# The first expert layer of a two-layer graph network: two phases with weights in two parts, on one Trainium2 core

## The reference, cut to what matters

```
x = x + _L0_ffn_ref(_layernorm(x), w1, b1, w2, b2, wr, br)
...
logits = xf @ wr + br
topk_vals, topk_idx = jax.lax.top_k(logits, K)             # K = 2 of E = 4
gates = jax.nn.softmax(topk_vals, axis=-1)
h = gelu(einsum('nd,edh->enh', xf, w1) + b1)               # 1024 -> 512
y = einsum('enh,ehd->end', h, w2) + b2                     # 512 -> 1024
c = einsum('eh,ehd->ed', gelu(b1), w2) + b2
out = einsum('nk,nkd->nd', gates, y_sel - c_sel + c.sum(axis=0))
```

## Time and profile before

| what | us |
|---|---|
| median of 3 runs | 2559.07 (2556.42 to 2559.77) |
| the profiled execution's own time | 2577.34 |
| its span, first to last instruction | 2575.3 |
| mean granted TensorE clock (share of full speed) | 0.971 |
| PE / DVE / ACT / POOL busy | 2397.2 / 1564.5 / 920.4 / 887.0 |

### The profile page before, as it was taken

The page is one execution under the profiler, slowest core; times in us unless marked ns, Lnnn a source line. Parts: engine busy times, 40 slices in busy tenths (PEclk is TensorE's granted clock), DMA queues, the critical chain, the costliest instruction groups (busy, mean ns, idle before and its releaser), DMA issues.

```text
span 2575.3 us, 29106 instructions
## 1 busy us (share of the span) xinstructions
PE 2397.2 (93%) x9625; PEld 1694.6 (66%) x9625; DVE 1564.5 (61%) x2417; ACT 920.4 (36%) x1629; POOL 887.0 (34%) x843
## 2 busy tenths in 40 slices
PE   6989998969999979999999999999999898977997
PEld 3543334634444458788888888887778676866785
DVE  8737776421142376645545555558889889766555
ACT  4012223311111233221221221228789896533333
POOL 2757774001111035655600000034346552213443
PEclk9999999979999989999999999999999999988998
DMA  4026676273343275454354354268678794457864
GB/s 155 1 97 205 205 208 172 111 255 100 109 126 98 65 258 192 171 193 143 123 192 144 121 191 151 106 237 258 212 250 295 273 344 161 142 181 285 325 217 169
DMA packets 195723, 466.10 MB, mean 181 GB/s; under 512 B 29352, under 2 KB 30152, under 8 KB 195608
## 3 DMA queue, kind: packets, MB, share of 16 engines
q1 hardware_dynamic: 101192, 219.34, 24.8%
q0 software_dynamic: 64272, 190.20, 23.1%
q10 hardware_dynamic: 30144, 55.12, 5.7%
HBM read 370.23 MB, written 99.96 MB: 183 GB/s over the span
## 4 chain that ended last, share of the span: by engine, by line
PE 76%; DMA 9%; DVE 6%; issue 4%; POOL 2%; ACT 2%; DVEq 0%; SPq 0%; ACTq 0%; POOLq 0%
PE pair L1292 8%; PE pair L1294 8%; PE pair L1293 8%; PE pair L1172 6%; PE pair L1192 6%; PE pair L1079 4%; DMA tok_x<-x_rows,tok_list 3%; PE pair L1310 3%; PE pair L1039 3%; PE pair L1313 3%; PE pair L1058 3%; PE pair L1330 3%; PE pair L1331 2%; PE pair L1332 2%; DMA tok_raw<-in_L_ffn_w 2%
## 5 line engine op out<-in xcount | busy, mean ns | idle before, releaser
L1471 ACT ACTIVATE sq_h<-quad 128x512 fp32r<-128x512 f32 x196 | 123.1, 634 | 453.6 <-PE pair L1294 448.8
L932 POOL DMA_INDIRECT rows_y<-y_rows,l_row x184 | 208.4, 1133 | 209.9 <-PE pair L1313 182.2
L1292 PE MATMUL pair<-sq_h,xh 128*128 128x512 f32 x700 | 273.3, 390 | 2.7 <-DVE sq_l L2294 2.7
L1294 PE MATMUL pair<-sq_l,xh 128*128 128x512 f32 x700 | 273.0, 390 | 0.0
L1293 PE MATMUL pair<-sq_h,xl 128*128 128x512 f32 x700 | 272.9, 390 | 0.0
L2382 DVE SCALAR_TENSOR_TENSOR low_y<-rows_y,l_inv,high_y 128x1024 fp32r<-128x1024 f32 x184 | 234.1, 1284 | 47.1 <-ACT high_y L1471 46.8
L1471 ACT ACTIVATE high_y<-rows_y,l_inv 128x1024 fp32r<-128x1024 f32 x184 | 210.4, 1144 | 40.9 <-PE pair L1313 27.5
L909 POOL DMA_INDIRECT inv_ring<-inv_count,at_ring x184 | 189.9, 1032 | 70.8 <-issue 52.5
L872 POOL DMA_INDIRECT XT<-h_rows,l_src x184 | 178.8, 972 | 70.0 <-issue 37.5
L2294 DVE TENSOR_TENSOR sq_l<-quad,sq_h 128x512 fp32r<-128x512 f32 x196 | 131.6, 696 | 97.8 <-ACT sq_h L1471 97.0
L1079 PE MATMUL pair<-XT,XN 128*128 128x504 f32 x368 | 188.8, 636 | 0.0
(11 more groups left out here) (369 smaller groups left out, 5055.6 us busy)
## 6 DMA issues: line engine op xcount, KB each, us to landing
quad<-in_L_gnn_weight SPq DMA_DIRECT2D x28, 1024.0 KB, 5.6
xh<-sum_parts SPq DMA_DIRECT2D x14, 1280.0 KB, 7.6
xl<-sum_parts SPq DMA_DIRECT2D x14, 1280.0 KB, 11.4
y_rows<-u ACTq DMA_DIRECT2D x70, 256.0 KB, 2.3
tok_raw<-in_L_ffn_w SPq DMA_DIRECT2D x8, 2048.0 KB, 13.5
tok_raw<-in_L_ffn_w SPq DMA_DIRECT2D x16, 1024.0 KB, 14.4
exp_bg<-bias_gelu_rows SPq DMA_DIRECT2D x23, 512.0 KB, 5.0
x_rows<-X SPq DMA_DIRECT2D x20, 512.0 KB, 6.5
```

The source lines that it names most:

```text
L932: pool.indirect_dma_start(rows_y[s % RING1][:], None, y_rows, bass.IndirectOffsetOnAxis(ap=l_row8[:, s:s + 1], axis=0)).then_inc(y_in[s % ...
L1292: mm(o, high[:, k, :], sq_h[:, k, :], start=(k == 0), stop=False)
L1294: last = mm(o, high[:, k, :], sq_l[:, k, :], start=False, stop=(k == KE - 1))
L1471: return nc.scalar.activation(dst, src, func, **kw)
```

## The change

The layer becomes two loops over the 23 slots. In the first PE makes all up products; ACT copies the raw product to `exp_h`, PE transposes it, DVE adds the bias on the transposed row (the bias is now one number per partition and slot, picked from a small table ahead of the loop), ACT takes the gelu and stores the slot's 128x512 hidden tile to `hidden_rows` in memory over its own DMA queue. In the second SP loads each hidden tile back (`load_hidden`), DVE takes gelu(b1) off (`take_bias`), ACT makes its high part (`hidden_parts`), DVE its low part (`hidden_low`), PE makes the down product, ACT copies it out (instead of DVE) into one of two buffers, POOL scatters it. Both products are made of three float32r matmuls. The gathered rows get a high part on ACT (`expert_x`) and a low part on DVE. Weights are split piece by piece (`expert_high` on ACT, `expert_low` on DVE, 64 pieces each, 128x512) into three places: w1 of experts 0, 1, 2 ahead of the loop or at its start, w1 of expert 3 at slot 9 into expert 0's place, w2 of expert 0 at slots 20 and 21, w2 of expert 1 right behind the last up product, w2 of expert 2 at slots 0 and 1 of the second loop, w2 of expert 3 at its slot 9. The constant row is summed in two banks of PSUM, a quarter at a time (first loop, slots 4 to 7 and 13 to 16; second loop, slots 2 and 3, and 4 to 7), copied out by ACT at slot 8 and summed by PE behind slot 9. The bias broadcasts, and the small transpose and store that fed them, go. The split of the first relation weight moves to slots 20 and 21 of the second loop.

```diff
-        exp_w = place("exp_w", "xt", [P, E0, 2, 8, HALF])
+        exp_raw = [place(f"exp_raw{i}", r, [P, 8, HALF], skip=8 * HALF) for i, r in enumerate(("xt", "u"))]
+        exp_tail = [place(f"exp_tail{h}", r, [P, KH, HALF], skip=16 * HALF) for h, r in enumerate(("xt", "u"))]
+        exp_w = place("exp_w", "xt", [P, 3, 20, HALF], F32R)
+        exp_x = place("exp_x", "os", [P, 3, 2, KH, P], F32R)
...
+        exp_hr = [place(f"exp_hr{b}", "xn", [P, KH, P], skip=D + b * HID) for b in range(2)]
+        exp_hp = [place(f"exp_hp{b}", r, [P, 2, KH, P], F32R, skip=n) for b, (r, n) in enumerate((("xn", 0), ("os", D)))]
+        exp_out = [place(f"exp_out{b}", r, [P, D]) for b, r in enumerate(("b2", "os"))]
+        c_kept = place("c_kept", "xt", [P, D], skip=16 * HALF)
...
+            def load_hidden(s):
+                sp.wait_ge(*hid_stored(s))
+                if s < 2:
+                    sp.wait_ge(exp_x_full, 2 * NT + 2 * (ESLOTS - 2) + 2)
...
+                    sp.wait_ge(exp_hl_ready, 1 + s - 1)
+                sp.dma_start(exp_hr[s % 2][:].rearrange("p c n -> p (c n)"), hid_dram[s]).then_inc(hid_in[s % 2][0], 16)
...
             sp.wait_ge(slot_summed, RING0 + SLOTS)
-            expert_half(0, 1)
+            first_weights(0, raw[:])
...
+            first_weights(1, exp_raw[1][:])
+            sp.wait_ge(a_full, A_ROUTE + len(TOKG))
+            first_weights(2, exp_raw[0][:])
+            sp.wait_ge(*exp_rows_here(0))
+            sp.wait_ge(*exp_rows_here(1))
+            sp.wait_ge(exp_wl_ready, 8)
+            first_weights(3, raw[:])
+            second_weights(0, tails)
+            sp.wait_ge(exp_wl_ready, 32)
+            second_weights(1, raw_halves)
+            load_hidden(0)
+            load_hidden(1)
+            sp.wait_ge(c_part_ready, 1)
+            sp.wait_ge(exp_wl_ready, 40)
+            second_weights(2, tails)
+            for s in range(2, ESLOTS):
+                load_hidden(s)
...
+            for s in range(2, ESLOTS):
+                pool.wait_ge(exp_x_full, 2 * NT + 2 * s - 2)
+                gather_expert(s)
...
+            def expert_up(s, j, at):
+                if j == 0:
+                    if s < 3:
+                        pe.wait_ge(exp_wl_ready, 8 * (s + 1))
+                    if s >= 2:
+                        pe.wait_ge(exp_h_ready, s - 1)
+                pe.wait_ge(exp_xl_ready, 2 * s + j + 1)
+                o = up_bank[s % 2]
+                high, low = exp_x[:, (2 * s + j) % 3, 0, :, :], exp_x[:, (2 * s + j) % 3, 1, :, :]
+                for c in range(KH):
+                    k = 4 * j + c
+                    if s == ONE_EXPERT:
+                        pe.wait_ge(exp_wl_ready, 24 + k + 1)
+                    w_high, w_low = (exp_w[:, bass.ds(at, 1), n, :].rearrange("p o n -> p (o n)") for n in (k, 8 + k))
+                    mm(o, high[:, c, :], w_high, start=(k == 0), stop=False)
+                    mm(o, low[:, c, :], w_high, start=False, stop=False)
+                    last = mm(o, high[:, c, :], w_low, start=False, stop=(k == KD - 1))
+                    if k == KD - 1:
+                        last.then_inc(exp_up_full, 1)
+                    elif s in (ONE_EXPERT - 1, ESLOTS - 1):
+                        last.then_inc(exp_piece_free, 1)
...
+            def expert_down(s, h, at):
+                if h == 0:
+                    if s == 0:
+                        pe.wait_ge(exp_wl_ready, 40)
+                    pe.wait_ge(exp_hl_ready, 1 + s + 1)
+                if s >= 2:
+                    pe.wait_ge(exp_out_ready, 2 * (s - 2) + h + 1)
+                elif s == 1:
+                    pe.wait_ge(exp_h_ready, ESLOTS - 1)
+                o = exp_down[s % 2][h]
+                high, low = exp_hp[s % 2][:, 0, :, :], exp_hp[s % 2][:, 1, :, :]
+                for k in range(KH):
+                    piece = h * KH + k
+                    if s in (1, 2, ONE_EXPERT):
+                        pe.wait_ge(exp_wl_ready, {1: 40, 2: 48, ONE_EXPERT: 56}[s] + piece + 1)
+                    w_high, w_low = (exp_w[:, bass.ds(at, 1), n, :].rearrange("p o n -> p (o n)") for n in (piece, 8 + piece))
+                    mm(o, high[:, k, :], w_high, start=(k == 0), stop=False)
+                    mm(o, low[:, k, :], w_high, start=False, stop=False)
+                    last = mm(o, high[:, k, :], w_low, start=False, stop=(k == KH - 1))
...
+            pe.wait_ge(exp_at_ready, 1)
+            expert_rows(0)
+            expert_rows(1)
+            for s in range(ESLOTS):
+                at = place_of(exp_up_at, s)
+                for j in range(2):
+                    if s + 1 < ESLOTS:
+                        expert_rows(2 * s + 2 + j)
+                    expert_up(s, j, at)
+                    if j == 0 and s >= 1:
+                        expert_hidden(s - 1)
+            for s in range(ESLOTS):
+                at = place_of(exp_down_at, s)
                 for h in range(2):
-                    if s >= 1:
-                        pe.wait_ge(exp_out_ready, 2 * s + h - 1)
-                    for k in range(KH):
-                        last = mm(down_bank[h][:], exp_hT[:, k, :], exp_w[:, bass.ds(exp_index[s % 2], 1), 1, h * KH + k, :].rearrange("p o n -> p (o n)"),
-                                  start=(k == 0), stop=(k == KH - 1))
-                    last.then_inc(exp_down_full, 1)
-
-            pe.wait_ge(exp_of_ready, 1)
-            expert_rows(0)
-            for s in range(ESLOTS):
-                expert_up(s)
-                if s + 1 < ESLOTS:
-                    expert_rows(s + 1)
-                if s >= 1:
-                    expert_down(s - 1)
-                expert_hidden(s)
+                    expert_down(s, h, at)
+                    if s == 0 and h == 0:
+                        expert_hidden(ESLOTS - 1)
...
+            def expert_high(src, at, pieces):
+                for k in pieces:
+                    copy(exp_w[:, at, k, :], src[k]).then_inc(exp_wh_ready, 1)
...
+            for e, at in ((1, 1), (2, 0)):
+                act.wait_ge(exp_w_in[e], 16)
+                expert_high([exp_raw[at][:, k, :] for k in range(KD)], at, range(KD))
+
+            def expert_x(n):
+                act.wait_ge(exp_x_full, 2 * NT + n + 1)
+                copy(exp_x[:, n % 3, 0, :, :], tx_bank[n % 2][:].rearrange("p (q n) -> p q n", q=4)).then_inc(exp_xT_ready, 1)
+
+            def keep_h(s):
+                act.wait_ge(exp_up_full, s + 1)
+                if s >= 1:
+                    act.wait_ge(exp_h_full, s)
+                copy(exp_h[:], up_bank[s % 2][:]).then_inc(exp_h_ready, 1)
+
+            def store_h(s):
+                act.wait_ge(exp_hm_ready, s + 1)
+                nc.scalar.activation(exp_hT[s % 2][:], exp_hT[s % 2][:], ACT.Gelu).then_inc(exp_gelu_ready, 1)
+                act.wait_ge(exp_gelu_ready, s + 1)
+                act.dma_start(hid_dram[s], exp_hT[s % 2][:].rearrange("p c n -> p (c n)")).then_inc(hid_out[s % 2][0], 16)
+
+            def hidden_parts(s):
+                act.wait_ge(exp_hb_ready, 1 + s + 1)
+                if s >= 2:
+                    act.wait_ge(exp_down_full, 2 * (s - 2) + 2)
+                copy(exp_hp[s % 2][:, 0, :, :], exp_hr[s % 2][:]).then_inc(exp_hh_ready, 1)
+
+            expert_x(0)
+            expert_x(1)
...
+                if s >= 1:
+                    keep_h(s - 1)
...
+                else:
+                    hidden_parts(0)
+                    hidden_parts(1)
+                if s >= 1:
+                    store_h(s - 1)
...
+            act.wait_ge(exp_w_in[1], 48)
+            for k in range(KD):
+                if k < KD - 1:
+                    act.wait_ge(exp_piece_free, KD - 1 + k + 1)
+                else:
+                    act.wait_ge(exp_up_full, ESLOTS)
+                expert_high(in_raw, 2, [k])
+            keep_h(ESLOTS - 1)
...
+            for s in range(ESLOTS):
+                if 1 <= s < ESLOTS - 1:
+                    hidden_parts(s + 1)
+                if s == 0:
+                    store_h(ESLOTS - 1)
+                    act.wait_ge(exp_w_in[2], 48)
+                if s in (0, 1):
+                    expert_high(in_tails, 0, range(4 * s, 4 * s + 4))
...
+                    act.wait_ge(exp_down_full, 2 * s + h + 1)
+                    if s >= 2 and h == 0:
+                        act.wait_ge(*put_here(s - 2))
+                    copy(exp_out[s % 2][:, h * HALF:(h + 1) * HALF], exp_down[s % 2][h][:]).then_inc(exp_out_ready, 1)
...
+            def expert_low(src, at, pieces):
+                for k in pieces:
+                    expert_low_count[0] += 1
+                    dve.wait_ge(exp_wh_ready, 1 + expert_low_count[0])
+                    v.tensor_tensor(exp_w[:, at, 8 + k, :], src[k], exp_w[:, at, k, :].bitcast(F32), ALU.subtract).then_inc(exp_wl_ready, 1)
...
+            dve.wait_ge(gelu_b_ready, 1)
```

(109 more changed lines are left out.)

286 lines of the change are left out of this document (136 added, 150 removed).

## The result

The changed kernel takes **2504.24 us** (median of 4 runs, 2497.97 to 2505.64); the kernel before, run beside it, 2559.42 (4 runs, 2556.42 to 2561.09). The ratio is 0.9769, 95% interval 0.9749 to 0.9790, so 54 to 64 us less; the medians lie 55 apart. The forecast was 2495.9 with a range of 2488 to 2514.

What follows compares the result with a forecast made beforehand. PE was taken as the layer's bound. Terms -66.1 + 0.6 + 0.4 - 2.2 + 3.4 + 1.0 - 0.3 gave -63.2, taken off the 2559.07 us median: 2495.9, range 2488 to 2514.

Steps and rivals of the forecast that it cites:

- The products: Layer's 368 up and down products on PE: three float32r matmuls at 0.679 us replace one float32 at 0.859; -66.1 us.
- Rival 1: PE's split matmuls run at 0.215 us each, a product costs 0.644, the layer 79 less: 2483 us; chance 0.04.
- The head: Layer start: added DVE operations make the list 0.6 us late; splitting rows delays the first up product by 0.4.
- The waits that go: PE's waits of 1.4 us for the first hidden row and 0.77 for the last disappear: -2.2 us.
- the end: Layer's end: ACT copies out right behind PE, since DVE's split of the relation weight has moved; -0.3 us.
- The seam: Between the loops: PE stands at slot 22's transposes for ACT's copy behind eight weight pieces; +3.4 us (0 to +7).
- After the seam: Early second loop: a slow hidden load holds up DVE's low part and so down(3); +1.0 us (0 to +8).
- The loops: In both loops PE covers ACT's and DVE's work, including the splits at slot 9; 0 us (0 to +5).
- rival 4: Order on ACT and DVE: each of four late weight splits holds up PE by 4 us; +16, 2512; chance 0.10.
- the 2.2 that the forecast had: First loop's gathers on POOL: needed 9.5 us after release, landing after 4.2 to 7.3, so covered by 2.2.
- Rival 2: Second loop: hidden tile's memory round trip outlasts PE's 5.44 us slot from landing 3.9; chance 0.07, past break-even 0.04.

Runs made afterwards that it cites:

- e_rt: The changed kernel with every hidden tile loaded twice, the second load waiting for the first and DVE for the second: 2536.04 us, ratio 0.9894 to the kernel before.
- e_seam: The changed kernel with ACT's copy of slot 22's up product ahead of the eight weight pieces: 2662.64 us, ratio 0.9781 to the kernel before.
- e_rt_low: Hidden tiles loaded twice as in e_rt, with DVE's low part of tile s+1 ahead of the bias of tile s+2: 2500.54 us, ratio 0.9747.
- e_static: The changed kernel with each slot's weight place written into the code, not computed at run time: 2507.93 us, ratio 0.9780 to the kernel before.
- e_f32: The changed kernel's two phases with one float32 matmul per product, low parts made but unused: 2731.49 us, ratio 1.0031 to the kernel before.

## Why the forecast came out as it did

**The products (-66.1) were right in kind and 2 too large.** The 368 products are the whole gain: 63.8 us between the two-phase kernel with float32 products and the change. A slot of the second loop is 5.44 as worked out. One of the first is 6.84 and not 6.76, 1.8 over 23 slots, because the matmuls there are 0.229 apart while those of the second loop and of the relation stage hold 0.227. Computed addresses are not the cause; what is stays open. Rival 1 (0.215 a matmul) did not happen. The rule named with it in the Trainium skill, "TensorE: Matmul & The Clock Gate", section "Back-to-back issue gap", gives 216 ns for a warm matmul by itself and 131 for a stream of them with weight loads. The traces have 227 and 229 for float32r with a weight load each, so the measurement decides, against both.

**The head (+0.6 and +0.4).** From list product to gather it is 6.53 now and was 5.85: +0.7. The first low part cost next to nothing: 8.25 from gather to first product against 8.21 in the first pair of profiles, 8.28 against 7.98 in the second.

**The waits that go (-2.2) and the end (-0.3)** hold: PE has no wait for a hidden row within the first loop, and the last scatter comes 1.4 behind the last matmul instead of 1.6, so 0.2 and not 0.3.

**The seam (+3.4)** was right in place and mechanism, ACT's copy behind eight weight pieces, and measured 2.4. What the forecast missed is that it was not ACT's order alone: taking the copy forward moved the stop to down(2), since DVE was as late. Four pieces moved into the idle time of both engines removed it.

**After the seam (+1.0)** is 0: down(3) does not wait. The one wait for DVE, 0.2, stands at down(0). **The loops (0)** held for ACT and DVE: the four late splits (rival 4) never stopped PE. The gathers were not quite covered by the 2.2 that the forecast had: PE stands for a second one, 0.8 in the repeated profile of the change and 1.0 in that with constant addresses. The loops did not hold for the clock: 1.6 behind the constant row's products in the first profile, which no term had.

Added up with what was measured: -64.3 + 0.7 + 0 - 2.2 + 2.4 + 0.2 - 0.2 + 1.6 = -61.8, against the 61.4 that the layer lost. That the forecast's 63.2 comes so near is in part luck: the products and the clock cost 3.4 more than it had, the head, the seam and what follows it about 2 less.

**Rival 2, the round trip**, was the right one to fear. Its formula (landing plus 1.6) holds within 0.25, at 4.07 for a landing of 2.68 and 7.50 for 6.14. The landing of 3.9 from which it decides follows from it; no run put the landings there. It did not strike because the landing was 2.9, as the row of 256 KB in the stage behind had it, and not the 5.0 of the earlier trace rows. The section "Issuing engines are not separate DMA queues" of the Trainium skill, "DMA: Bandwidth & Descriptors", spoke against the change, and no price for it shows: 23 more loads changed the layer by nothing once DVE's order allowed it. Scatters do land in 4.6 and not 3.4, but in 3.8 with the hidden tiles loaded twice and in 3.5 with two matmuls a product, where the DMA share is no lower (0.48 and 0.56), so that more traffic makes them slower is not shown.

**From the layer to the whole.** The whole lost 55 by the medians (54 to 64 by the ratio's interval), the layer 61 to 64. The forecast of 2495.9 is 8 too low: some 2 are the layer's, the other 6 lie outside it. The stage from the last gate tile to the end took 287.1, 284.8 (where near 279 was expected) and 281.6 in the three profiles with float32 products, and 274.9 to 286.0 in the nine others. That is a scatter of the size in question, with the two groups overlapping. Whether the change costs something in other stages is neither shown nor excluded.

## What to carry to other kernels

Where one engine is busy in all of a stage and the others in a third of it, a change that makes this engine's work cheaper by splitting operands on the others can be worth its arithmetic: here the added work came to nothing as long as each loop of waits was shorter than a slot. Write each such loop down with its period: here one instruction out of order on DVE made a loop over two buffers come round once per tile instead of once in two, which cost nothing at 5.44 us a slot, 32 us when the load was doubled, and 11 when PE's slot was 3.62. A stop at a seam can run through two engines: here mending the order on one only moved it, and moving work on both into their idle time took it away.

## What the runs showed of the hardware

- Float32r matmuls with a weight load each are 0.227 apart in one loop and 0.229 to 0.230 in another of the same shapes, in every profile with three matmuls a product, with and without computed addresses.
- After a stop of PE the matmuls can run 0.43 apart, the 1.2 GHz level. They did behind stops of 1.8 and 1.9 us (e_rt, e_seam) and of 2.4 (e_rt_low), and did not behind 2.4 (both profiles of the change) and 2.5 (e_static). The same came with no stop at all behind four float32 products (two of them with K = 4) in three of the ten profiles with two phases (the first of the change, e_f32, e_rt), for up to 3.6 us; in the seven others the granted clock stayed at 1.00.
- The indirect scatter's time on POOL has two levels, and its median went from 1.00 to 1.31 us with the change. It does not follow the traffic: it is 0.97 again with the hidden tiles loaded twice and with two matmuls a product. In the first profile of the change each of the 17 scatters of 1.3 us or more starts beside DVE's subtraction for the low part of a hidden tile, which reads two tiles in SBUF, and none of the six shorter ones does so from its start; in the kernel before, the two of 1.39 stand beside DVE's sums of the constant row. That DVE's reads are the cause was not tried.
